# Long scans over a feature-major tile, their multipliers in PSUM, and the layer 1 sum on TensorE

## The chip, the cores and the metric

The kernel runs on one core of one Trainium2 chip. The metric is the device time of one execution in microseconds (us), from the first to the last instruction; lower is better. All data are float32 unless said otherwise. The engines are called as in the profile: PE (TensorE), PEld (its weight loads), DVE (VectorE), ACT (ScalarE), POOL (GpSimd, which here issues the indirect DMAs) and SP (which issues the plain ones).

## The reference

A graph network of two layers over 12500 nodes and 200000 edges sorted by receiver `dst`. Each layer's result is added to its input and normalised.

```
# layer 0: attention over incoming edges, 4 heads of 16 features
h = (x @ W_node).reshape(n, H, HD)
attn = a_src[src] + a_dst[dst] + edge_attr_16 @ W_edge       # a_src = h . attn_src, a_dst = h . attn_dst
attn = where(attn >= 0, attn, 0.2 * attn)
attn_max = zeros(n, H).at[dst].max(attn)
attn = exp(attn - attn_max[dst])
attn_sum = zeros(n, H).at[dst].add(attn)
out = zeros(n, H, HD).at[dst].add(h[src] * (attn / (attn_sum[dst] + 1e-8)))
x = layernorm(x + layernorm(out + h) * gamma + beta)
# layer 1: a message per edge, its mean per receiver
hid = relu(concat(x[src], x[dst], edge_attr_32) @ W1 + b1)   # 160 -> 128
agg = segment_sum(hid @ W2 + b2, dst) / max(degree, 1)
x = layernorm(x + agg + (x @ Wn + bn))
```

## The kernel before

**Lanes.** The edges are padded to 128 lanes of 1568 columns (`LANE`): partition p holds edges 1568 p to 1568 p + 1567, sorted by receiver. A sum or maximum per receiver is a running one along the lane: `same` (128 x 1568) is 1 where an edge has the receiver of the one before it and 0 where a new receiver starts. The running rows are stored to DRAM (`rows0`, `rows1`), and the last row of each node is later fetched from there. What a receiver has in the lanes before is carried over by small matmuls.

**Stages, in order of time.** (1) The node table `table0` (h, source terms) is made, and the edges of each node are counted. (2) Layer 0 over the edges: `K0` = 49 chunks of `C0` = 32 columns. (3) Layer 0 over the nodes, 10 steps: combine, normalise, project to `table1s` (source part of W1) and `table1d` (receiver part), and scatter the latter to the first edge of each receiver in `recv_term`, which is zero elsewhere. (4) Layer 1 over the edges: `K1` = 196 chunks of `C1` = 8 columns. (5) Layer 1 over the nodes.

**Gathers.** A column of 128 source rows is fetched by one indirect DMA of POOL: L433 and L450 for layer 0 (`gather0`, `gather_columns`, 1440 + 128 of them), L525 for layer 1 (`gather1`, 1568). Each layer has a ring of four slots (`G0`, `G1`), and POOL fills a slot again when its last user has raised a semaphore: `rows0_ready` (the last scan of a chunk) in layer 0, `relu_done` in layer 1. L484 fetches last rows of nodes (`gather_last`), L489 scatters receiver terms.

**A chunk of layer 0** (`turn0` of DVE, L1025 to L1060). DVE adds three terms to a score (L1035, L1038), takes the leaky relu (L1040), scans the maximum per head (L1044, four scans of 32), forms the arguments of two exponentials (L1047 to L1049), which ACT computes in one pass (L748). DVE multiplies the second by `same` (L1051), the gathered features by the first (L1053, 128 x 2048, in place), and runs 64 + 4 scans of 32 columns (L1057, L1059), each `row = decay * row_before + term`, into `R0[par]`; SP stores that (1152 KB). PE multiplies the edge attributes (4 small matmuls); SP also writes 2 MB of zeros to `recv_term` a chunk.

**A chunk of layer 1** (`turn1` of DVE, L1178 to L1215). SP loads the receiver terms into one of four `X1` buffers. DVE runs two recurrences over the eight columns, one instruction of 128 x 128 for a column each, the two interleaved: the receiver rows (L1191, `X[u] = same[u] * X[u-1] + X[u]`), and the sums of the chunk before (L1197, the same form on `H1`). Then it adds the receiver rows to the gathered rows (L1209, 128 x 1024) and the PE result, which is in PSUM (L1214, two of 128 x 512); ACT takes relu into `H1` (L832), SP stores `H1` (512 KB). PE multiplies the edge attributes with a block-diagonal W1 (two matmuls of 128x512 f32, L565, a helper's line).

**What sets the order** is written by hand: each engine has its own loop, with semaphores between them, and SP's loop per chunk (`chunk0`, `chunk1`) loads and stores in a fixed order, so a load stands behind the store before it.

## Time and profile before

| | |
|---|---|
| runs | 4751.53, 4755.95, 4757.55 us; median 4755.95 |
| profiled execution, span | 4755.7 us |
| busy: POOL, DVE, PE, PEld, ACT | 3565.7, 2619.7, 1308.6, 660.9, 493.5 us |
| layer 0 gathers of the loop | 358.5 to 2257.6 us |
| layer 1 gathers | 2589.9 to 4585.5 us |
| mean granted TensorE clock | 0.554 |

Times in the trace count from the first instruction. A row of a group gives the line, engine, operation, output <- inputs, shapes, count, busy time, the mean of one instruction in ns, and behind the last bar the idle time of the engine just before these instructions, with what ended it ("issue": nothing that the profile shows). A timeline row gives start, duration, line and, in brackets, the idle time before. A fp32 matmul appears as two MATMUL instructions.

### The profile page before, as it was taken

Reading aid. Unit: us, or ns where it says so; the run is one execution under the profiler, and the core shown is the slowest. Engines: PE = TensorE matmul, PEld = TensorE weight load, DVE = VectorE, ACT = ScalarE, POOL = GpSimd, SP = SyncE. Lnnn points to the kernel's source line nnn. Section 1 sums busy time; section 2 is a strip of 40 time slices with the busy share of each in tenths; the row PEclk is TensorE's granted clock in tenths of the full one; section 3 lists DMA queues with packets and bytes.
Section 4 is the critical chain, followed back from the end, with each engine's and each line's share of the span. In section 5 each row is a group of like instructions: output and inputs, shape, how many; then the busy total and the mean of one; then the engine's idle time right before and its main releaser. Section 6 shows DMA issues by size and latency. Waiting matters only on the chain. (4 is left out here: it accounts for less than half of the span.)

```text
span 4755.7 us, 33914 instructions
## 1 busy us (share of the span) xinstructions
PE 1308.6 (28%) x3363; PEld 660.9 (14%) x3363; DVE 2619.7 (55%) x8568; ACT 493.5 (10%) x1011; POOL 3565.7 (75%) x3558
## 2 busy tenths in 40 slices
PE   7600000000000000000575333333333333333336
PEld 4300000000000000000453111111111111111126
DVE  6545443344433444433774666666666666666645
ACT  4500000000000000000232111111111111111101
POOL 5777777777777777777676777777777777777766
PEclk9855555555555555555555655655665556556655
DMA  3034333333333333333232555555555555555532
GB/s 124 10 112 160 100 105 118 118 117 112 93 118 118 118 118 99 106 118 113 85 121 94 169 171 167 165 170 170 162 170 171 161 170 171 166 166 171 170 104 63
DMA packets 240932, 622.28 MB, mean 131 GB/s; under 512 B 74956, under 2 KB 102543, under 8 KB 221521
## 3 DMA queue, kind: packets, MB, share of 16 engines
q1 hardware_dynamic: 127568, 443.81, 28.2%
q0 software_dynamic: 113280, 177.74, 14.7%
q14 instruction: 78, 0.63, 0.0%
q8 instruction: 6, 0.10, 0.0%
HBM read 328.11 MB, written 293.29 MB: 131 GB/s over the span
## 5 line engine op out<-in xcount | busy, mean ns | idle before, releaser
L525 POOL DMA_INDIRECT edge_arena<-table1s,ix x1568 | 1518.0, 968 | 477.9 <-issue 435.2
L433 POOL DMA_INDIRECT edge_arena<-table,ix x1440 | 1460.5, 1014 | 438.9 <-issue 438.9
L565 PE MATMUL ps<-w1e_bd,edge_terms 128*128 128x512 f32 x784 | 725.1, 1080 | 1264.4 <-DMA edge_terms<-e32g_d 1264.4
L1191 DVE SCALAR_TENSOR_TENSOR edge_arena<-edge_arena,same 128x128 f32<-128x128 f32 x1568 | 542.0, 346 | 263.6 <-issue 189.1
L565 PE MATMUL ps<-we_bd,edge_terms 128*128 128x32 f32 x392 | 93.6, 403 | 1864.1 <-DVE score L1038 1803.8
L1035 DVE TENSOR_TENSOR score<-edge_arena,node_wide 128x128 f32<-128x128 f32 x49 | 14.2, 291 | 1066.0 <-DMA edge_arena<-table,ix 1065.6
L1057 DVE TENSOR_TENSOR_SCAN edge_arena<-wq,edge_arena 128x32 f32<-128x32 f32 x3136 | 586.8, 268 | 1.8
L1197 DVE SCALAR_TENSOR_TENSOR edge_arena<-edge_arena,same 128x128 f32<-128x128 f32 x1568 | 539.7, 344 | 1.5 <-ACT edge_arena L832 1.2
L565 PEld LDWEIGHTS ps<-w1e_bd,edge_terms 128*128 128x128 f32 x784 | 229.0, 322 | 1759.2 <-issue 1759.2
L1209 DVE TENSOR_TENSOR edge_arena<-edge_arena 128x1024 f32<-128x1024 f32 x196 | 240.9, 1229 | 404.5 <-DMA edge_arena<-table1s,ix 404.5
L832 ACT ACTIVATE edge_arena<-edge_arena 128x1024 f32<-128x1024 f32 x196 | 207.0, 1056 | 1800.9 <-DVE edge_arena L1214 1800.9
L565 PEld LDWEIGHTS ps<-we_bd,edge_terms 128*128 128x128 f32 x392 | 87.2, 328 | 1870.5 <-DVE score L1038 1769.3
L484 POOL DMA_INDIRECT node_arena<-rows,end_ix x200 | 210.5, 1053 | 96.5 <-issue 59.4
L1214 DVE TENSOR_TENSOR edge_arena<-edge_arena,ps 128x512 f32<-128x512 f32 x392 | 251.8, 683 | 6.7
L748 ACT ACTIVATE wq<-expo 128x256 f32<-128x256 f32 x49 | 20.4, 416 | 2028.3 <-DVE expo L1049 2028.3
L450 POOL DMA_INDIRECT edge_arena<-table,ix x128 | 143.3, 1120 | 39.0 <-issue 39.0
L489 POOL DMA_INDIRECT recv_term<-node_arena,start_ix x100 | 120.6, 1206 | 48.4 <-issue 32.7
L565 PE MATMUL ps<-node_arena 128*128 128x512 bf16 (+1 forms) x800 | 146.3, 332 | 28.5 <-DVE row_base L953 16.4
L565 PE MATMUL ps<-w1n,node_arena 128*128 128x128 f32 (+1 forms) x400 | 133.9, 488 | 24.1 <-ACT node_arena L777 24.1
L455 POOL DMA_INDIRECT dst_term<-a_dst,start_idx x100 | 104.9, 1049 | 30.5 <-issue 30.5
L742 ACT ACTIVATE node_arena<-ps,node_half 128x1057 bf16<-128x1057 f32 x100 | 114.3, 1143 | 63.4 <-PE ps L565 58.9
L1053 DVE TENSOR_TENSOR edge_arena<-edge_arena,wq 128x2048 f32<-128x2048 f32 x49 | 111.9, 2284 | 0.0
(177 smaller groups left out, 1462.5 us busy)
## 6 DMA issues: line engine op xcount, KB each, us to landing
recv_term<-zeros SPq DMA_DIRECT2D x98, 1024.0 KB, 9.1
edge_arena<-recv_term SPq DMA_DIRECT2D x196, 512.0 KB, 4.1
rows<-edge_arena SPq DMA_DIRECT2D x196, 512.0 KB, 5.1
rows<-edge_arena SPq DMA_DIRECT2D x49, 1152.0 KB, 4.4
edge_arena<-table,ix POOLq DMA_INDIRECT x1568
edge_terms<-e32g_d SPq DMA_DIRECT2D x196, 128.0 KB, 4.8
edge_arena<-table1s,ix POOLq DMA_INDIRECT x1568
edge_terms<-e16g_d SPq DMA_DIRECT2D x49, 256.0 KB, 9.2
```

The source lines that it names most:

```text
L433: pool.indirect_dma_start(G0[slot][:, u, :], None, table0, bass.IndirectOffsetOnAxis(ap=ix[slot][:, u:u + 1], axis=0)).then_inc(gathered0[ ...
L450: pool.indirect_dma_start(G0[slot][:, u, :], None, table0, bass.IndirectOffsetOnAxis(ap=ix[slot][:, u:u + 1], axis=0)).then_inc(gathered0[ ...
L484: pool.indirect_dma_start(RG[r][:, b, :], None, rows, bass.IndirectOffsetOnAxis(ap=end_ix[r][:, b:b + 1], axis=0)).then_inc(done[r], 16)
L489: pool.indirect_dma_start(recv_term, bass.IndirectOffsetOnAxis(ap=start_ix[r][:, b:b + 1], axis=0), PDs[r][:, b, :], None, bounds_check=NE ...
L525: pool.indirect_dma_start(G1[slot][:, u, :], None, table1s, bass.IndirectOffsetOnAxis(ap=ix[slot][:, u:u + 1], axis=0)).then_inc(gathered1 ...
L565: return pe.matmul(out_, lhsT, rhs, start=start, stop=stop)
L832: act.activation(H1[s], G1[s], ACT.Relu).then_inc(relu_done, 1)
L1057: scan(R[:, :, f], wq[:, :, H + f // HD], G[:, :, f], before[:, f:f + 1], ALU.mult, ALU.add)
L1191: stt(X[:, u, :], X[:, u - 1, :] if u else Xb[:, C1 - 1, :], same[:, bass.ds(c * C1 + u, 1)], X[:, u, :], ALU.mult, ALU.add).then_inc(dv1, 1)
L1197: a = stt(Hc[:, u, :], Hc[:, u - 1, :] if u else Hb[:, C1 - 1, :], same[:, bass.ds(c * C1 - C1 + u, 1)], Hc[:, u, :], ALU.mult, ALU.add)
L1209: tt(G1[s], G1[s], X, ALU.add).then_inc(recv_used, 1)
L1214: last = tt(part_g, part_g, ps[:, 2 * s + g, :], ALU.add)
```

## The change

In both layers the many short instructions of a recurrence become scans over a long free axis. A tile is laid out feature-major, with one more column in front of each feature's columns: the seed, which is the last column of the chunk before. A scan `state = mult * state + data` runs over all features in one instruction; the multiplier at a seed column is 0, which starts the next feature.

**Layer 0.** `F0[par]` (4 heads x 17 x 33, 17 being 16 features and the sum of weights) lies in the node arena, in two copies. The maximum is one scan of 132 elements with multipliers `hold0` in SBUF (a copy of `same` by ACT). ACT writes the weights (exp of 128 elements) to PSUM, again into `F0`'s 17th row, and the decays, spread over 17 rows (2176 elements), to PSUM (`decay`, from bank 2 on); the product with `same` is gone, the argument being lowered by up to 1000 instead (`cut`, ALU.min). DVE multiplies features by weights (2048 elements, now SBUF times PSUM, into `F0`), and runs one scan of 2244 elements, multipliers in PSUM. ACT copies `F0` and the maxima into `R0` for the store. POOL's slot is free after the multiply (`g0_free`) rather than after the scans.

**Layer 1.** A chunk is 16 columns (`C1`), so there are 98. There is one `X1` buffer (1 MB a load) in the node arena; ACT copies it feature-major into `F1[0]` or `F1[1]`, DVE scans it in five pieces (4 of 510 elements, 1 of 136), with multipliers in PSUM (`hold1`, written by ACT). PE adds the three terms in PSUM banks 2 to 5: four edge matmuls, four of the identity with the gathered rows, four of the identity with the scanned receiver rows (read with a stride). ACT's relu reads PSUM and writes `F1[2]` or `F1[3]`; DVE scans that too, and ACT copies it into `H1`, which is stored (1 MB). Both adds of DVE (L1209, L1214) are gone. SP and POOL wait for DVE to leave the node arena (`arena_free`).

The diff, cut to its core, in the order globals and tiles, SP, PE, ACT (layer 0, then 1), DVE (layer 0, then 1):

```diff
-C1 = 8
+C1 = 16
+CUT = 1000.0
...
+        decay = ps_flat[:, 2 * BANK:2 * BANK + H * HF * T0]
+        weight = ps[:, 7, 0:H * C0].rearrange("p (h t) -> p h t", t=C0)
...
+        T1 = C1 + 1
+        F1 = [part(node_arena, i * HID * T1, HID * T1) for i in range(4)]
+        XF1, HF1 = (0, 1), (2, 3)
+        X1 = part(node_arena, 4 * HID * T1, C1, HID)
+        FEATS = BANK // T1
+        hold1 = [ps[:, r, 0:FEATS * T1] for r in range(2)]
+        PIECES1 = [(f * T1, min(HID, f + FEATS) * T1) for f in range(0, HID, FEATS)]
...
+            def chunk1(c, s, loads=True, follows=True, stores=True):
+                if follows:
+                    sp.wait_ge(xf_ready, c + 1)
+                    sp.dma_start(X1, recv_p[:, bass.ds(c * C1 + C1, C1), :]).then_inc(recv_in, 16)
                 if loads:
+                    sp.wait_ge(edge1_mm, c * 2 + 4)
+                    sp.dma_start(edge_terms[s][:, :, :], e32g[:, bass.ds(c * 4 + 4 * RING1, 4), :]).then_inc(e32_in[s], 16)
+                if stores:
+                    store1(c - 1, 1 - s % 2)
...
             def edge1(c, s, it):
+                r = s % 2
                 pe.wait_ge(e32_in[s], it * 16 + 16)
-                pe.wait_ge(pre_ready, c + 1)
-                for g in range(2):
-                    last = mm(ps[:, 2 * s + g, :], edge_terms[s][:, g, :], w1e_bd[:, :])
-                last.then_inc(edge1_mm, 1)
+                pe.wait_ge(half_used[0], c + 1)
+                for g in range(4):
+                    mm(ps[:, 2 + g, :], edge_terms[s][:, g, :], w1e_bd[:, :], True, False)
+                pe.wait_ge(gathered1[s], it * (16 * C1) + 16 * C1)
+                for g in range(4):
+                    mm(ps[:, 2 + g, :], ident[:, :], G1[s][:, 4 * g:4 * g + 4, :].rearrange("p t f -> p (t f)"), False, False)
+                pe.wait_ge(scanned_x, c + 1)
+                for g in range(4):
+                    recv = F1_f[XF1[r]][:, :, 1 + 4 * g:5 + 4 * g].rearrange("p f t -> p t f")
+                    last = mm(ps[:, 2 + g, :].rearrange("p (t f) -> p t f", f=HID), ident[:, :], recv, False, True)
+                    if g % 2:
+                        last.then_inc(edge1_mm, 1)
...
+            def turn0(c, slot, copies, holds):
+                act.wait_ge(weight_arg, c + 1)
+                act.activation(weight, expo[:, 0, :, :], ACT.Exp).then_inc(weights_ready, 1)
+                act.wait_ge(rows0_ready, c + 1)
+                act.activation(F0_h[par][:, :, HD, 1:T0], expo[:, 0, :, :], ACT.Exp)
+                act.wait_ge(decay_arg, c + 1)
+                act.wait_ge(scanned0, c + 1)
+                act.activation(decay_h[:, :, :, 1:T0], expo[:, 1, :, :].unsqueeze(2).to_broadcast([P, H, HF, C0]),
+                               ACT.Exp).then_inc(decay_ready, 1)
...
+                act.wait_ge(scanned0, c + 2)
+                act.wait_ge(rows0_stored[par], (c - par) * 8 + 16)
+                act.activation(heads(R0[par][:, :, 0:D]), F0_h[par][:, :, 0:HD, 1:T0], ACT.Copy)
...
+            def turn1(c, s, copies=True, follows=True, c_later=True):
+                if follows:
+                    act.wait_ge(led_x, c + 1)
+                    act.wait_ge(edge1_mm, c * 2 + 2)
+                    recv_1(c + 1, 1 - r)
+                if c_later:
+                    rows_1(c - 1, 1 - r)
+                    if follows:
+                        hold_1(c + 1, 1 - r)
+                act.wait_ge(edge1_mm, c * 2 + 4)
...
+                act.activation(F1_f[HF1[r]][:, :, 1:T1].rearrange("p f t -> p t f"),
+                               ps[:, 2:6, :].rearrange("p a (t f) -> p (a t) f", f=HID), ACT.Relu).then_inc(half_used[0], 1)
...
-                tt(wq[:, :, H:2 * H], wq[:, :, H:2 * H], wide(same_c.unsqueeze(2), [P, C0, H]), ALU.mult)
-                tt(feats, feats, wide(wq[:, :, 0:H].unsqueeze(3), [P, C0, H, HD]), ALU.mult).then_inc(dv0, 1)
-                for f in range(D):
-                    scan(R[:, :, f], wq[:, :, H + f // HD], G[:, :, f], before[:, f:f + 1], ALU.mult, ALU.add)
+                scan(flat(M), flat(hold0[par]), flat(score), 0.0, ALU.mult, ALU.max).then_inc(dv0, 1)
...
+                tt(F[:, :, 0:HD, 1:T0], G[:, :, 0:D].rearrange("p t (h d) -> p h d t", d=HD),
+                   wide(weight.unsqueeze(2), [P, H, HD, C0]), ALU.mult).then_inc(g0_free, 1)
...
+                scan(F0[par], decay, F0[par], 0.0, ALU.mult, ALU.add).then_inc(scanned0, 1)
...
+            def scan1(F, hold, done):
+                for lo, hi in PIECES1:
+                    last = scan(F[:, lo:hi], hold[:, 0:hi - lo], F[:, lo:hi], 0.0, ALU.mult, ALU.add)
+                last.then_inc(done, 1)
...
+            def turn1(c, s, it, first=False):
+                    dve.tensor_copy(F1_f[XF1[r]][:, :, 0:1], F1_f[XF1[1 - r]][:, :, C1:T1]).then_inc(led_x, 1)
+                    lead1(c - 1, 1 - r)
...
+                scan1(F1[XF1[r]], hold1[r], scanned_x)
+                if not first:
+                    sums1(c - 1, 1 - r)
```

## Rows read from the trace of the kernel before

**Rows 1.** The page, part 1: busy us (share of the span) x instructions.

```profile
PE 1308.6 (28%) x3363; PEld 660.9 (14%) x3363; DVE 2619.7 (55%) x8568; ACT 493.5 (10%) x1011; POOL 3565.7 (75%) x3558
```

**Rows 2.** Groups of the whole span, POOL's three largest kinds of gather.

```profile
L525 POOL DMA_INDIRECT edge_arena<-table1s,ix x1568 | 1518.0, 968 | 477.9 <-issue 435.2 <-ACT edge_arena L832 42.1 <-ACT ix L726 0.6
L433 POOL DMA_INDIRECT edge_arena<-table,ix x1440 | 1460.5, 1014 | 438.9 <-issue 438.9
...
L450 POOL DMA_INDIRECT edge_arena<-table,ix x128 | 143.3, 1120 | 39.0 <-issue 39.0
```

**Rows 3.** Groups of POOL in a stretch of layer 0 with DVE idle.

```profile
L433 POOL DMA_INDIRECT edge_arena<-table,ix x17 | 16.0, 943 | 5.2 <-issue 5.2
```

**Rows 4.** Timeline of layer 0: a gather beside the multiply of L1053.

```profile
489.97 2.28 DVE L1053 TENSOR_TENSOR edge_arena<-edge_arena,wq 128x2048 f32<-128x2048 f32 x1
490.33 2.74 POOL L433 DMA_INDIRECT edge_arena<-table,ix  x1 [0.30 <-issue]
```

**Rows 5.** Timeline before layer 0's chunks: a gather beside L1021's scans.

```profile
299.83 13.61 DVE L1021 TENSOR_TENSOR_SCAN node_wide<-same,lane_rows,node_wide 128x1568 f32<-128x1568 f32 x4 [76.48 <-DMA node_wide<-dst_term]
300.22 3.85 POOL L450 DMA_INDIRECT edge_arena<-table,ix  x1 [0.30 <-issue]
```

**Rows 6.** Timeline of stages 4 and 5: gathers beside DVE instructions that read PSUM.

```profile
2907.25 1.28 DVE L1214 TENSOR_TENSOR edge_arena<-edge_arena,ps 128x512 f32<-128x512 f32 x2
...
2908.33 0.95 POOL L525 DMA_INDIRECT edge_arena<-table1s,ix  x1 [0.31 <-issue]
...
4650.02 0.82 DVE L1244 TENSOR_TENSOR node_arena<-ps,inv_deg 128x640 f32<-128x640 f32 x1
4650.53 0.94 POOL L484 DMA_INDIRECT node_arena<-rows,end_ix  x1 [0.30 <-issue]
```

**Rows 7.** Groups of the whole span: the short scans of layer 0.

```profile
L1057 DVE TENSOR_TENSOR_SCAN edge_arena<-wq,edge_arena 128x32 f32<-128x32 f32 x3136 | 586.8, 268 | 1.8
```

**Rows 8.** Timeline of the end of layer 0's edge stage.

```profile
2256.61 0.94 POOL L433 DMA_INDIRECT edge_arena<-table,ix  x1 [0.30 <-issue]
2259.08 0.29 DVE L1035 TENSOR_TENSOR score<-edge_arena,node_wide 128x128 f32<-128x128 f32 x1 [23.76 <-DMA edge_arena<-table,ix]
...
2264.51 11.97 DVE L1057 TENSOR_TENSOR_SCAN edge_arena<-wq,edge_arena 128x32 f32<-128x32 f32 x64
2276.40 0.82 DVE L1059 TENSOR_TENSOR_SCAN edge_arena<-wq,edge_arena 128x32 f32<-128x32 f32 x4
...
2281.74 0.94 POOL L484 DMA_INDIRECT node_arena<-rows,end_ix  x1 [24.18 <-DMA rows<-edge_arena]
```

**Rows 9.** Groups of ACT, whole span: relu and the exponentials.

```profile
L832 ACT ACTIVATE edge_arena<-edge_arena 128x1024 f32<-128x1024 f32 x196 | 207.0, 1056 | 1800.9 <-DVE edge_arena L1214 1800.9
...
L748 ACT ACTIVATE wq<-expo 128x256 f32<-128x256 f32 x49 | 20.4, 416 | 2028.3 <-DVE expo L1049 2028.3
```

**Rows 10.** Timeline before layer 1: eight edge matmuls in a row.

```profile
2567.72 8.82 PE L565 MATMUL ps<-w1e_bd,edge_terms 128*128 128x512 f32 x16 [4.31 <-DMA edge_terms<-e32g_d]
```

**Rows 11.** Windows: stretch, engines' busy us (x), PEclk, DMA share, GB/s.

```profile
2567.70:2571.10 3.40, 3.38 (x4) 1.51 (x5) 3.40 (x1) 0.00 (x0) 3.40 (x1) 0.50 0.30 90
2571.10:2576.50 5.40, 5.40 (x13) 2.09 (x11) 5.37 (x2) 0.00 (x0) 5.09 (x2) 0.99 0.04 12
```

**Rows 12.** The page, part 6: a DMA of 1 MB, issue to landing.

```profile
recv_term<-zeros SPq DMA_DIRECT2D x98, 1024.0 KB, 9.1
```

**Rows 13.** Timeline where layer 1's edge stage begins.

```profile
2571.68 6.82 DVE L1169 TENSOR_TENSOR node_wide<-node_wide,node_arena 128x6400 f32<-128x6400 f32 x1
...
2588.59 0.98 POOL L531 DMA_INDIRECT edge_arena<-table1d,ends_i  x1 [0.31 <-issue]
```

**Rows 14.** Timeline of the end of layer 1's edge stage.

```profile
4584.57 0.94 POOL L525 DMA_INDIRECT edge_arena<-table1s,ix  x1 [0.30 <-issue]
4587.18 1.23 DVE L1209 TENSOR_TENSOR edge_arena<-edge_arena 128x1024 f32<-128x1024 f32 x1 [3.73 <-DMA edge_arena<-table1s,ix]
...
4597.49 0.94 POOL L484 DMA_INDIRECT node_arena<-rows,end_ix  x1 [11.97 <-DMA rows<-edge_arena]
```

More of the change, by code:

```diff
@@ L205, in build @@
         rstd = part(node_arena, 11716, NC)
+        HF = HD + 1
+        F0 = [part(node_arena, r * H * HF * T0, H * HF * T0) for r in range(2)]
+        F0_h = [f.rearrange("p (h d t) -> p h d t", d=HF, t=T0) for f in F0]
+        ps_flat = ps[:, :, :].rearrange("p a b -> p (a b)")
+        decay = ps_flat[:, 2 * BANK:2 * BANK + H * HF * T0]
+        decay_h = decay.rearrange("p (h d t) -> p h d t", d=HF, t=T0)
+        weight = ps[:, 7, 0:H * C0].rearrange("p (h t) -> p h t", t=C0)
+        cut = part(node_arena, 9296, LANE)
         big_a = part(node_arena, 4160, H, P)
@@ L407, in _ @@
             pool.memset(zeros[:, :], 0.0)
+            for r in range(2):
+                pool.memset(hold0[r][:, :, :], 0.0)
             pool.memset(upto[:, 0:1], 0.0)
@@ L743, in _, with hold @@
                                    scale=-1.0, accum_out=sign_sum[:, bass.ds(j * 2 + i, 1)]).then_inc(row_free[i], 1)
[L746 to L748 removed]
+            def hold(c, par):
+                act.activation(hold0[par][:, :, 1:T0], same[:, bass.ds(c * C0, C0)].unsqueeze(1).to_broadcast([P, H, C0]),
+                               ACT.Copy).then_inc(hold0_ready, 1)
@@ L752, in _ @@
+                act.activation(R0[par][:, :, MCOL:ROW].rearrange("p t h -> p h t"), peak[par][:, :, 1:T0],
+                               ACT.Copy).then_inc(rows0_ready, 1)
+            act.wait_ge(seeds_zero, 1)
+            for par in range(2):
+                hold(par, par)
             with act.Fori(0, (K0 - 5) // RING0) as it:
                 for slot in range(RING0):
-                    turn0(it * RING0 + slot, slot, True)
+                    turn0(it * RING0 + slot, slot, True, True)
@@ L876, in _ @@
             dve.sem_inc(cc_free, 1)
-            dve.sem_inc(pre_ready, RING1)
+            for h in range(2):
+                dve.sem_inc(half_used[h], 1)
             dve.sem_inc(agg_used, 2)
@@ L1053, in turn0 @@
-                tt(feats, feats, wide(wq[:, :, 0:H].unsqueeze(3), [P, C0, H, HD]), ALU.mult).then_inc(dv0, 1)
-                dve.wait_ge(dv0, c * 4 + 4)
-                dve.wait_ge(rows0_ready, c + 1)
-                for f in range(D):
-                    scan(R[:, :, f], wq[:, :, H + f // HD], G[:, :, f], before[:, f:f + 1], ALU.mult, ALU.add)
-                for h in range(H):
-                    last = scan(R[:, :, ZCOL + h], wq[:, :, H + h], wq[:, :, h], before[:, ZCOL + h:ZCOL + h + 1], ALU.mult, ALU.add)
@@ L1231, in _ @@
             dve.wait_ge(carry1_mm, 1)
+            for r in range(2):
+                dve.wait_ge(rows1_stored[r], 16 * (K1 // 2 + 1))
             dve.tensor_copy(rgT[0][:, 0:P], ps[:, 0, 0:P]).then_inc(carry1_cp, 1)
```

247 lines of the change are left out of this document (135 added, 112 removed).

## The prediction

> **What bounds the kernel now.** I read the page's first part and its groups first. POOL is busy 75% of the span [rows 1], but that counts only the 0.94 to 1.01 us that each indirect DMA takes to generate; behind each of them stand about 0.305 us of issue in which POOL does nothing else. With both, the layer 1 gathers take 1518.0 + 477.9 = 1995.9 us, the layer 0 gathers of the loop 1460.5 + 438.9 = 1899.4 us and the first 128 gathers 143.3 + 39.0 = 182.3 us [rows 2]: 4077.6 of 4755.7 us. The reader is to see that the idle time in these rows is all "issue" (the 42.1 us put down to ACT in layer 1 are the same 0.3 us gaps, since 477.9 / 1568 = 0.305): POOL never waits for DVE, ACT, PE or a landing. So DVE's 2619.7 us, which the change cuts most, are worth nothing as such. What is worth something is what DVE does to the gathers.
>
> For that I take a gather alone. In a stretch of layer 0 in which DVE is idle, 17 gathers have a mean of 943 ns [rows 3]; over all of the layer the mean is 1014 ns, in layer 1 it is 968 ns [rows 2]. The timeline shows where the rest comes from: the gather of 490.33 starts while the feature multiply of L1053 runs (489.97 to 492.25), and takes 2.74 us; it ends at 493.07, 0.82 us after the multiply has ended [rows 4]. The same with a scan: the first L1021 scan (1568 elements) starts at 299.83, and the gather that starts 0.39 us later takes 3.85 us [rows 5]. So a gather that begins during a DVE instruction with both inputs in SBUF stops 0.12 us into its work until DVE is done, and then needs its other 0.82 us. A gather that began just before such an instruction isn't held. Where one of the inputs is in PSUM it is different: the gather of 4650.53 begins inside L1244 (PSUM times SBUF, 4650.02 to 4650.84) and takes 0.94 us where the rule above would give 1.13; the one of 2908.33 begins 0.2 us before the L1214 pair (SBUF plus PSUM) is done and takes 0.95 us [rows 6].
>
> The Trainium skill (SBUF — State Buffer, section "Who interferes with whom") says that a DVE instruction with two SBUF inputs contends with a GpSimd instruction that reads SBUF, and that one with at most one SBUF input outside the 2-port modes doesn't; our rows agree. In the same list it reports a probe in which tensor_tensor did not stall descriptor generation. That sentence speaks against any gain here: without the stalls there would be nothing to win, and the time would be the one that I give below for "nothing to win". The 2.74 us row decides against it.
>
> **The change, part by part.** The span is 4755.7 us, the median of the runs 4755.95: what I take off the one I take off the other.
>
> Layer 0, gathers. Excess over the free gather: 1460.5 − 1440 × 0.943 = 102.6 us, and 143.3 − 128 × 0.943 = 22.6 us for the first 128, of which most belongs to L1021 and the counting stage and stays. The multiply of L1053 runs 49 times, 46 of them beside the gathers of the loop and three beside the first 128. It can cost 0 (no gather begins in it) to some 2.2 us, and cost 1.8 at 490.33; taking 2.28 less half of the 1.25 us between gathers, 1.65, it carries 46 × 1.65 = 76 us of the 102.6, and the rest is small delays by the L1057 scans; of the first 128 it carries 3 × 1.65 = 5 us. In the new kernel the multiply reads its weights from PSUM, and the 68 short scans become one of 4 × 17 × 33 = 2244 elements with its multipliers in PSUM. By rows 6 neither holds a gather. Left are two-SBUF instructions of 128 elements as before, which did next to nothing, and one scan of 132 elements; I leave 4 us for them (between 0, and 0.5 us a chunk = 24 us). Gain: 102.6 + 5 − 4 = 103.6 us.
>
> Does the new work fit behind a chunk of gathers, 32 × (0.943 + 0.305) = 39.9 us? Scan: L1057 takes 268 ns for 32 elements [rows 7] and the four L1021 scans 13.61 us, 3.40 us each for 1568 [rows 5], so (3.40 − 0.19) / 1536 = 2.09 ns an element (0.19 us being the start-to-start time of the short ones, 11.97 / 64 [rows 8]), and 2244 elements take 4.9 us. With the multiply (2.3) and eight small instructions DVE has about 10 us a chunk. ACT: L832 takes 1056 ns for 1024 elements and L748 416 ns for 256 [rows 9]: 0.83 ns an element and 0.2 us. Two exponentials of 128, the decay of 2176, the copies of 2048 and 2 × 128, the hold and the indices come to 0.3 + 0.3 + 2.0 + 1.9 + 0.6 + 0.5 = 5.6 us. Both hidden; if that cover were gone, each us of either would cost 49 us.
>
> Layer 1, gathers. Excess: 1518.0 − 1568 × 0.943 = 39.4 us, from the 32 short instructions a chunk with a pointer scalar and two SBUF inputs. The new scans read their holds from PSUM, the two adds of DVE are gone. I leave 1 us (0 to 10): gain 38.4 us.
>
> Layer 1, does it fit behind 16 gathers, 16 × 1.248 = 20.0 us? DVE: 2 × 2176 elements in 10 scans, 2 × (4.55 + 5 × 0.12) = 10.3 us, and two seeds. ACT: three passes of 2048 (1.9 us each), a hold of 480 (0.6) and the indices (0.2): 6.5 us. PE: four edge matmuls, four for the gathered rows, four for the receiver rows, all 128x512 f32. The trace has eight such matmuls back to back (16 instructions, 8.82 us) [rows 10]: the first 3.4 us at a granted clock of 0.50 (1.2 GHz), in which four instructions are done, then 0.99 (2.4 GHz) with the other twelve in 5.4 us [rows 11]. A matmul is two instructions: 1.7 us at the lower level and 0.87 at the higher. Twelve cost 20.4 us or 10.4 us. PSUM has one buffer for them, so relu (1.9 us) and the hand-overs (0.3) come on top: 12.6 us at the higher clock. After the gathers of a chunk have landed PE does eight matmuls without a pause, longer than the 3.4 us after which the clock rose; I take two at the lower level and six at the higher, 8.6 us, then relu, then four edge matmuls: 14 us of 20. Matmuls that read the receiver rows with a stride of 17 elements stand in no row; at twice the time they add 3.5 us and stay hidden. The receiver rows now have one buffer, and SP loads chunk c+1 only behind ACT's copy of chunk c and behind the store of chunk c−2, which waits for ACT again. 1 MB takes 9.1 us to land at the worst [rows 12]; with recv copy, rows copy, hold and relu (6.3 us) this loop takes some 16 us, under 20. POOL's slots: four of 16 columns, freed by relu; it is three chunks (60 us) ahead.
>
> Where layer 1 begins, SP and POOL now wait for DVE to leave the node arena. DVE's last pass there ends at 2578.50 and POOL comes to the first gather of layer 1's stage at 2588.59 [rows 13], so I cost it at nothing (0 to 2 us); without these 10 us it would cost what DVE is late.
>
> The end of layer 0. Before: the last gather begins at 2256.61, DVE starts at 2259.08 and its last scan ends at 2277.22, and POOL goes on at 2281.74, 4.5 us later with the store between [rows 8]. New, from 2259.08: three small (1.0), the scan of 132 (0.5), the subtraction (0.3), ACT's exponential (0.4), multiply (2.3), scan (4.9), ACT's copies (2.4), store (4.5): 16.3 us in place of 22.7, gain 6.4 us.
>
> The end of layer 1. Before: the last gather begins at 4584.57, DVE starts at 4587.18, POOL goes on at 4597.49: 10.3 us [rows 14]. New: eight matmuls from the lower clock (8.6), relu (2.1), five scans (5.2), ACT's copy into the rows (2.0), a store of 1 MB (4.4, like the 1.15 MB of layer 0): 22.3 us with 0.2 for hand-overs. Loss 12.2 us (10 at the higher clock throughout, 17 at the lower).
>
> Sum: 4755.7 − 103.6 − 38.4 − 6.4 + 12.2 = **4619.5 us**, by 2.9% less. The node stages are left alone: nothing in their code changes.
>
> **The rivals.**
> 1. A scan with its multipliers in PSUM still holds gathers. Rows 6 show tensor_tensor alone, and not a scan; what speaks for it is only that the rows are short instructions of another kind. Price: as L1053 cost 1.6 us with 2.28, a scan of 4.9 us costs about 4.3, × 49 = 209 us; in layer 1 ten scans a chunk, each holding the gather that begins in it by half of 1.06 us, some 6 gathers a chunk: 2.8 × 98 = 275 us. 4619.5 + 209 + 275 = 5104 us, slower than before. It decides as soon as half of the scans hold a gather (142 us gained against 484). Chance 0.07.
> 2. PE stays at its lower clock and becomes the bound of layer 1: 20.4 + 1.9 + 0.3 = 22.6 us a chunk against 20.0, 98 × 2.6 = 255 us, 4619.5 + 255 + 5 = 4880 us, slower. It decides from 20 us a chunk for twelve matmuls and a relu. Against it stands the 0.99 of [rows 11] after 3.4 us of the same matmuls. The Trainium skill (TensorE: Matmul & The Clock Gate, Part 1) says that half rate is the default and activity releases it, which would end this case by itself: a PE that is the bound is busy all the time. Chance 0.03.
> 3. The loop through the one receiver buffer and the hand-overs of ACT, DVE and SP is longer than 20 us: at 22 us a chunk 98 × 2 = 196 us, 4815 us, slower; at 20.5 us 4670 us. It needs landings of over 13 us for 1 MB, which no row shows. Chance 0.06, half of it slower than before.
> 4. Nothing to win: the stalls come back at other places, or don't hang on DVE's inputs at all. Then the ends alone count: 4755.7 − 6.4 + 12.2 = 4761.5, within 0.2%. Chance 0.03.
>
> **How the numbers follow.** The forecast has 0.81. Its own bounds: 24 us more for the small layer 0 instructions, 9 for layer 1, 5 for the end at the lower clock, some us of what I couldn't see; below, 4 + 1 for what I left and 2 for the end. That is 4610 to 4655. The range goes to 4675 to take in the mild half of case 3 and hand-overs that I mis-sized, and down to 4600. Faster by over 0.2% (about what a measurement of this kernel can tell from no change): 0.81 + 0.03 (the mild half of case 3) = 0.84; slower: 0.07 + 0.03 + 0.03 = 0.13; between: case 4, 0.03.
>
> **What would show it.** Right: the mean of the gathers at 943 to 950 ns in both layers, all idle time before them still "issue" at 0.305 us; a gather that begins during a long scan takes 0.94 us. DVE's busy time falls by over a third with no effect of its own. Between the last gather of layer 1 and the first of the last stage about 25 us in place of 12.9. Wrong: gathers of 3 to 5 us beside the 2244-element scan (case 1); idle time of POOL released by ACT's relu, with PE at 0.50 (case 2) or with PE waiting for the scan of the receiver rows (case 3).

## The result, and the profile after

The changed kernel takes 4681.82 us (median; 4679.21 to 4683.91) against 4754.67 us for the kernel before in the same measurement: a ratio of 0.9849, with a 95% interval of 0.9835 to 0.9863. It is faster by 1.5%, where 2.9% were forecast, and 6.8 us above the upper end of the range. The profiled execution has a span of 4680.6 us, 75.1 less than before. The medians here and below leave out one execution, of the kernel of experiment 5, which took 9870.74 us where its other three took 4625 to 4635.

The page's first part and POOL's largest groups (columns as in [rows 1] and [rows 2]):

```profile
PE 2215.4 (47%) x4911; PEld 966.5 (21%) x4931; DVE 1959.1 (42%) x2644; ACT 1758.3 (38%) x1403; POOL 3425.6 (73%) x3560
...
L557 POOL DMA_INDIRECT edge_arena<-table1s,ix x1568 | 1480.9, 944 | 486.3 <-issue 478.2
L465 POOL DMA_INDIRECT edge_arena<-table,ix x1440 | 1361.3, 945 | 438.8 <-issue 438.8
```

POOL's waits in the whole span (us in total, times, longest):

```profile
POOL edge_arena L557 <- issue: 478.2, 1546, 1.5
POOL edge_arena L465 <- issue: 438.8, 1440, 0.3
POOL node_arena L516 <- DMA rows<-edge_arena: 95.4, 2, 73.8
```

The gathers did what was forecast: their means are 944 and 945 ns in place of 968 and 1014 [rows 2]. The time went into the last line: before the last stage POOL stands for 73.8 us, where it stood for 11.97 [rows 14]. The account of the span, before to after:

| Term | forecast | measured | from |
|---|---|---|---|
| Gathers of layer 0, with the first 128 | −103.6 | −104.9 | 1460.5 to 1361.3, and 143.3 to 137.6 (137.6 is the group of L482) |
| Gathers of layer 1, busy | −38.4 | −37.1 | 1518.0 to 1480.9 |
| Waits within layer 1's gathers | 0 | +8.4 | 477.9 to 486.3 |
| Wait at the end of layer 0 | −6.4 | −2.6 | 24.2 to 21.6 (95.4 − 73.8) |
| Wait at the end of layer 1 | +12.2 | +61.8 | 11.97 to 73.8 |
| Sum | −136.2 | −74.4 | span: −75.1 |

Two gathers beside the new work of DVE in layer 0 (timeline: start, us, engine, line):

```profile
996.03 3.83 DVE L1170 TENSOR_TENSOR node_arena<-edge_arena,ps 128x2048 f32<-128x2048 f32 x1
997.10 0.95 POOL L465 DMA_INDIRECT edge_arena<-table,ix  x1 [0.30 <-issue]
...
999.95 4.83 DVE L1175 TENSOR_TENSOR_SCAN node_arena<-ps,node_arena 128x2244 f32<-128x2244 f32 x1
1000.85 0.94 POOL L465 DMA_INDIRECT edge_arena<-table,ix  x1 [0.30 <-issue]
```

Both begin inside an instruction with its multipliers in PSUM, and neither is held, against 2.74 us in [rows 4].

Where the 73.8 us come from is seen in layer 1's loop (timeline; POOL and the weight loads left out):

```profile
3501.64 3.80 ACT L928 ACTIVATE node_arena<-ps 128x2048 f32<-128x2048 f32 x1 [3.15 <-PE ps L602]
...
3503.34 0.33 SPq L401 DMA_DIRECT2D node_arena<-recv_term  x1
3505.49 5.91 PE L602 MATMUL ps<-w1e_bd,edge_terms 128*128 128x512 f32 x8 [3.89 <-ACT node_arena L928]
...
3511.24 3.60 PE L602 MATMUL ps<-edge_arena,ident 128*128 128x512 f32 x8
3513.61 3.83 ACT L908 ACTIVATE node_arena<-node_arena 128x2048 f32<-128x2048 f32 x1 [7.76 <-DMA node_arena<-recv_term]
3514.67 7.41 PE L602 MATMUL ps<-node_arena,ident 128*128 128x512 f32 x8
...
3522.12 3.80 ACT L928 ACTIVATE node_arena<-ps 128x2048 f32<-128x2048 f32 x1 [0.64 <-PE ps L602]
```

Read the starts. From relu to relu it is 20.48 us: relu 3.80, edges 5.75, gathered rows 3.43, receiver rows 7.41, and 0.09 between them. Each waits for the one before it, as they share one set of PSUM banks. POOL needs 19.98 us for 16 gathers. PE and ACT thus fall 0.5 us behind in each of 98 chunks. For most of the layer nobody waits for that: POOL is ahead by the slots of the ring. The lag comes due at the end of the layer, when everything still in the ring has to pass through the loop, and from about the 80th chunk on POOL itself waits a little (the 8.4 us). Over the whole layer, from the first relu at 2515.7 to the last at 4505.2, the loop has a mean of 20.51 us.

Groups of the new passes (whole span; busy, mean ns); L809 and the scan L1175 came out as forecast, the others did not:

```profile
L602 PE MATMUL ps<-w1e_bd,edge_terms 128*128 128x512 f32 x784 | 580.0, 909 | 382.3 <-ACT node_arena L928 377.4 <-DMA edge_terms<-e32g_d 4.9
...
L908 ACT ACTIVATE node_arena<-node_arena 128x2048 f32<-128x2048 f32 x98 | 375.3, 3830 | 524.7 <-DMA node_arena<-recv_term 485.9 <-DVE node_arena L1314 38.4 <-ACT node_arena L928 0.4
L928 ACT ACTIVATE node_arena<-ps 128x2048 f32<-128x2048 f32 x98 | 372.3, 3799 | 324.5 <-PE ps L602 324.5
...
L817 ACT ACTIVATE edge_arena<-node_arena 128x2048 f32<-128x2048 f32 x49 | 189.8, 3874 | 319.7 <-DVE node_arena L1175 319.7
...
L809 ACT ACTIVATE ps<-expo 128x2176 f32<-128x2176 f32 x49 | 97.4, 1988 | 6.9 <-DVE expo L1165 1.8
...
L1175 DVE TENSOR_TENSOR_SCAN node_arena<-ps,node_arena 128x2244 f32<-128x2244 f32 x49 | 236.7, 4831 | 4.4
L1170 DVE TENSOR_TENSOR node_arena<-edge_arena,ps 128x2048 f32<-128x2048 f32 x49 | 187.8, 3833 | 0.0
```

L908 and L928 write a tile in SBUF with 17 elements from one to the next, L817 writes one with 72 (a row of `R0`), and they take 1.85 to 1.89 ns an element; L809, which writes neighbours, takes 0.91 and is at the forecast. The same on DVE: L1170, which reads the gathered rows 72 elements apart, takes 3.83 us where L1053 took 2.28 [rows 4].

TensorE's clock in the stretches of that loop (us, busy us of PE, PEld, DVE, ACT, POOL, PEclk, DMA share, GB/s):

```profile
3505.50:3509.00 3.50, 3.50 (x4) 1.50 (x5) 3.42 (x4) 0.22 (x1) 2.59 (x4) 0.50 0.94 318
3509.00:3511.20 2.20, 2.20 (x5) 0.94 (x4) 1.91 (x5) 0.00 (x0) 1.59 (x3) 0.78 0.78 294
3511.20:3514.60 3.40, 3.40 (x9) 1.52 (x8) 0.00 (x0) 0.99 (x1) 2.64 (x3) 1.00 0.30 89
```

After the 3.89 us in which PE stands for relu it starts again at 0.50 (1.2 GHz), so the edge matmuls, not the gathered ones, pay for the clock. It is so in every chunk: the edge matmuls are busy 580.0 us in 98 chunks, 5.92 us each, and 5.91 in the one above.

### The profile page after: what moved, and what is told of

Same layout as the page of the kernel before. It is cut to its first block, busy times and chain, and to the rows that moved or that the text cites. A ratio compares the mean times of both kernels' runs of the same rounds, so it can differ in the third digit from the quotient of the medians.

```text
span 4680.6 us, 24041 instructions
## 1 busy us (share of the span) xinstructions
PE 2215.4 (47%) x4911; PEld 966.5 (21%) x4931; DVE 1959.1 (42%) x2644; ACT 1758.3 (38%) x1403; POOL 3425.6 (73%) x3560
## 4 chain that ended last, share of the span: by engine, by line
POOL 39%; PE 37%; issue 13%; ACT 8%; DVE 1%; DMA 1%; SPq 0%; POOLq 0%; DVEq 0%; ACTq 0%
PE ps L602 37%; POOL edge_arena L465 29%; ACT node_arena L928 8%; POOL edge_arena L482 3%; POOL node_arena L516 2%; POOL dst_term L487 2%; POOL edge_arena L557 1%; POOL recv_term L521 1%; DMA node_arena<-rows,end_ix 0%; PE ps L756 0%; DMA table<-node_arena 0%; DMA edge_arena<-table1s,ix 0%; SPq L313 0%; PE ps L682 0%; DVE node_arena L1175 0%
## 5 line engine op out<-in xcount | busy, mean ns | idle before, releaser
L557 POOL DMA_INDIRECT edge_arena<-table1s,ix x1568 | 1480.9, 944 | 486.3 <-issue 478.2
L465 POOL DMA_INDIRECT edge_arena<-table,ix x1440 | 1361.3, 945 | 438.8 <-issue 438.8
L1296 DVE TENSOR_TENSOR_SCAN node_arena<-ps,node_arena 128x510 f32<-128x510 f32 (+1 forms) x980 | 956.2, 1043 | 1027.1 <-ACT ps L903 792.7
L602 PE MATMUL ps<-node_arena,ident 128*128 128x512 f32 x784 | 726.4, 1083 | 0.0
L908 ACT ACTIVATE node_arena<-node_arena 128x2048 f32<-128x2048 f32 x98 | 375.3, 3830 | 524.7 <-DMA node_arena<-recv_term 485.9
L928 ACT ACTIVATE node_arena<-ps 128x2048 f32<-128x2048 f32 x98 | 372.3, 3799 | 324.5 <-PE ps L602 324.5
L913 ACT ACTIVATE edge_arena<-node_arena 128x2048 f32<-128x2048 f32 x98 | 370.6, 3782 | 12.2 <-DVE node_arena L1296 12.2
L602 PE MATMUL ps<-edge_arena,ident 128*128 128x512 f32 x784 | 354.4, 595 | 38.2 <-DMA edge_arena<-table1s,ix 38.2
L516 POOL DMA_INDIRECT node_arena<-rows,end_ix x200 | 212.7, 1064 | 155.7 <-DMA rows<-edge_arena 95.4
L817 ACT ACTIVATE edge_arena<-node_arena 128x2048 f32<-128x2048 f32 x49 | 189.8, 3874 | 319.7 <-DVE node_arena L1175 319.7
L602 PEld LDWEIGHTS ps<-node_arena,ident 128*128 128x128 f32 x784 | 159.5, 203 | 457.5 <-issue 457.5
L1175 DVE TENSOR_TENSOR_SCAN node_arena<-ps,node_arena 128x2244 f32<-128x2244 f32 x49 | 236.7, 4831 | 4.4
L602 PEld LDWEIGHTS ps<-edge_arena,ident 128*128 128x128 f32 x784 | 149.4, 191 | 228.0 <-issue 186.6
L1170 DVE TENSOR_TENSOR node_arena<-edge_arena,ps 128x2048 f32<-128x2048 f32 x49 | 187.8, 3833 | 0.0
L482 POOL DMA_INDIRECT edge_arena<-table,ix x128 | 137.6, 1075 | 39.0 <-issue 39.0
```

Source lines behind the costliest of these rows:

```text
L465: pool.indirect_dma_start(G0[slot][:, u, :], None, table0, bass.IndirectOffsetOnAxis(ap=ix[slot][:, u:u + 1], axis=0)).then_inc(gathered0[ ...
L482: pool.indirect_dma_start(G0[slot][:, u, :], None, table0, bass.IndirectOffsetOnAxis(ap=ix[slot][:, u:u + 1], axis=0)).then_inc(gathered0[ ...
L516: pool.indirect_dma_start(RG[r][:, b, :], None, rows, bass.IndirectOffsetOnAxis(ap=end_ix[r][:, b:b + 1], axis=0)).then_inc(done[r], 16)
L557: pool.indirect_dma_start(G1[slot][:, u, :], None, table1s, bass.IndirectOffsetOnAxis(ap=ix[slot][:, u:u + 1], axis=0)).then_inc(gathered1 ...
L602: return pe.matmul(out_, lhsT, rhs, start=start, stop=stop)
L817: act.activation(heads(R0[par][:, :, 0:D]), F0_h[par][:, :, 0:HD, 1:T0], ACT.Copy)
```

## The experiments

The theory after the result: layer 1's loop through the PSUM banks is 20.5 us and hence the bound; what made it so is the strided access to SBUF, in relu and in PE's receiver matmuls. The rivals: the loop through the receiver buffer (SP's load, ACT's copy, the scan), and the granted clock alone. Besides, the gain of layer 0 is to be tied to its cause.

**1. Relu in two halves**, each with its semaphore, so that the next edge matmuls start behind the first.

```diff
-                pe.wait_ge(half_used[0], c + 1)
                 for g in range(4):
+                    if g % 2 == 0:
+                        pe.wait_ge(half_used[g // 2], c + 1)
...
+                for h in range(2):
+                    act.wait_ge(edge1_mm, c * 2 + 3 + h)
+                    act.activation(F1_f[HF1[r]][:, :, 1 + 8 * h:9 + 8 * h].rearrange("p f t -> p t f"),
+                                   ps[:, 2 + 2 * h:4 + 2 * h, :].rearrange("p a (t f) -> p (a t) f", f=HID),
+                                   ACT.Relu).then_inc(half_used[h], 1)
```

> One edit to the changed kernel, with the same result: relu of layer 1 in two passes of 1024 (PSUM banks 2-3, then 4-5), each raising its own semaphore, and PE's edge matmuls of the next chunk wait for the half that they write. Theory A (the bound of layer 1 is the loop PE 16.58 us, relu 3.80, hand-over 0.1 through the one PSUM buffer, 20.48 us a chunk against POOL's 19.98): the loop falls to PE's own time, about 15 to 16.5 us, the consumers no longer fall behind, and the wait of POOL before the last stage falls from 73.8 to about 30 us: 4680 - 44 - 8 = 4628 us. Rival B (the loop through the one receiver buffer, SP's order and ACT's two copies is the bound): the halves take only 1.9 us from every second chunk; at most 20 us, 4660 or more. Rival C (only the lower clock of PE holds it): PE no longer pauses for relu and so keeps 2.4 GHz; the edge matmuls would fall from 5.75 to 3.4 us, which alone gives 18.1 us and the same total as A, but with relu still in the loop.

Measured: 4632.86 us for 4628 expected, ratio 0.9741 (0.9725 to 0.9757). POOL's waits:

```profile
POOL edge_arena L557 <- issue: 477.8, 1568, 0.3
...
POOL node_arena L516 <- DMA rows<-edge_arena: 51.3, 2, 29.8
```

All 1568 idle times in layer 1 are issue again, and the last wait falls from 73.8 to 29.8 us. Not all of these 44.0 us are the lag: behind the last matmul only the second half of relu is left on the path,

```profile
4459.55 1.98 ACT L930 ACTIVATE node_arena<-ps 128x1024 f32<-128x1024 f32 x1 [1.59 <-PE ps L602]
```

in place of 3.80 us, which is worth 1.8. The lag is the other 42.2 and the 8.5 within the gathers, 50.7 us, where a loop of 20.51 us against 19.98 makes 52 in 98 chunks. The edit gives back 49 of the 62 us that were missing, and nothing about POOL or the gathers was touched. Rival B, which had at least 4660 us, is false. On C, the clock, this run says nothing, as both theories gave the same total.

**2. Layer 0 alone**: the changed layer 0 with the layer 1 of before.

> Layer 0 as changed, layer 1 as before (chunks of 8, DVE's recurrences, adds on DVE). By the traces the layer 0 part gains 99.3 us in the loop's gathers, 5.7 in the first 128 and 2.6 at the end of the stage: 4755.7 - 107.6 = 4648 us, faster than the whole change (4681.8). If instead the layer 1 part also gained over before, this one would come out above 4681.8 us.

Measured: 4644.08 us, 4 us under the expectation, ratio 0.9765 (0.9748 to 0.9781). Two groups of POOL:

```profile
L541 POOL DMA_INDIRECT edge_arena<-table1s,ix x1568 | 1514.4, 966 | 477.8 <-issue 436.3 <-ACT edge_arena L871 39.9 <-ACT ix L742 1.5
L449 POOL DMA_INDIRECT edge_arena<-table,ix x1440 | 1362.9, 946 | 438.7 <-issue 438.7
```

So the layer 1 part, as built, loses 4681.8 − 4644.1 = 37.7 us, although its gathers are faster; with relu in halves it wins 11.2.

**3. Two receiver buffers**, everything else as in the changed kernel.

```diff
-        X1 = part(node_arena, 4 * HID * T1, C1, HID)
+        X1 = [part(node_arena, 4 * HID * T1 + i * (W1R + HID), C1, HID) for i in range(2)]
...
-                    sp.dma_start(X1, recv_p[:, bass.ds(c * C1 + C1, C1), :]).then_inc(recv_in, 16)
+                    sp.dma_start(X1[s % 2], recv_p[:, bass.ds(c * C1 + 2 * C1, C1), :]).then_inc(recv_in[s % 2], 16)
```

> One edit to the changed kernel, with the same result: two receiver buffers in place of one, so that a load is issued a whole chunk earlier. Theory A: the loop through PSUM and relu stays 20.48 us a chunk, and the time stays at 4680 us within 5 us. Rival B (the receiver loop is the bound): the wait for the landing (485.9 us in ACT, 88 times) goes, the chunk falls under 20 us, and the time to about 4630 us.

Measured: 4687.1 us, ratio 0.9849 (0.9833 to 0.9866), the same ratio as the changed kernel's; the time is 7 us above the 4680 expected, 2 more than the 5 allowed, in another measurement. Waits of ACT (L929 is relu) and of POOL:

```profile
ACT node_arena L929 <- PE ps L603: 736.4, 98, 22.9
...
POOL node_arena L517 <- DMA rows<-edge_arena: 95.4, 2, 73.8
```

ACT's wait for the receiver rows to land was 485.9 us and is 14.6 now; its wait for PE rose from 324.5 to 736.4 instead, and the end stayed at 73.8. The 485.9 us was the largest wait of ACT in the loop, and was worth nothing. The receiver loop, which the forecast had as its rival, was not the bound.

**4. Relu writes neighbouring elements.** Same amount of work and the same waits; the order of the features is left out, so the sums are of the wrong values.

```diff
-                act.activation(F1_f[HF1[r]][:, :, 1:T1].rearrange("p f t -> p t f"),
-                               ps[:, 2:6, :].rearrange("p a (t f) -> p (a t) f", f=HID), ACT.Relu).then_inc(half_used[0], 1)
+                act.activation(F1_f[HF1[r]][:, :, 1:T1],
+                               ps[:, 2:6, :].rearrange("p a b -> p (a b)").rearrange("p (f t) -> p f t", t=C1),
+                               ACT.Relu).then_inc(half_used[0], 1)
```

> One edit to the changed kernel: relu of layer 1 writes its 2048 results in runs of 16 neighbours (it leaves out the transposition to feature-major order, so the sums are of the wrong values). Theory A with a stride as the cause of ACT's 1.85 ns an element: relu takes 1.9 us in place of 3.80, the loop 18.6 us, under POOL's 20.0, and the time falls to about 4630 us. If the source in PSUM, not the stride of the write, costs the time: relu stays 3.8 us and the time 4680 us.

Measured: 4630.97 us, ratio 0.9736 (0.9717 to 0.9756). The group of relu:

```profile
L928 ACT ACTIVATE node_arena<-ps 128x2048 f32<-128x2048 f32 x98 | 183.9, 1876 | 276.4 <-PE ps L602 276.3
```

1876 ns is the 1.9 us that the forecast had put in, and with it the layer runs at POOL's pace: all 1568 idle times of POOL are issue, and the last wait is 28.6 us. The price of the strided write is shown. The run also decides on the clock alone. The edge matmuls are still slow,

```profile
L602 PE MATMUL ps<-w1e_bd,edge_terms 128*128 128x512 f32 x784 | 552.5, 871 | 197.7 <-ACT node_arena L928 192.8 <-DMA edge_terms<-e32g_d 4.9
```

871 ns an instruction against 909, and POOL doesn't wait: the setback of the clock by itself doesn't make the loop too long.

**5. PE reads the receiver rows as neighbours.**

```diff
-                    recv = F1_f[XF1[r]][:, :, 1 + 4 * g:5 + 4 * g].rearrange("p f t -> p t f")
-                    last = mm(ps[:, 2 + g, :].rearrange("p (t f) -> p t f", f=HID), ident[:, :], recv, False, True)
+                    recv = F1[XF1[r]][:, g * BANK:g * BANK + BANK]
+                    last = mm(ps[:, 2 + g, :], ident[:, :], recv, False, True)
```

> The same kernel as e4_receiver_unit_stride once more (the first time the kernel before itself took 5641 us on that chip in place of 4755, with waits that belong to no instruction, so that the few per cent in question drowned). PE reads the receiver rows as neighbouring elements; this leaves out their right order. Theory A (the loop through the one set of PSUM banks is the bound of layer 1): 4628 to 4633 us, no wait of POOL in the loop. Rival (the receiver loop of 20.15 us is right behind it): 4648 us or above.

Measured: 4633.21 us (4625.26 to 4635.43), ratio 0.9730 (0.9712 to 0.9748). This is just above the 4628 to 4633 of the theory, in a measurement in which the kernel before took 4763.5 us, 9 more than in 1. The group of the receiver matmuls, and POOL's waits:

```profile
L602 PE MATMUL ps<-node_arena,ident 128*128 128x512 f32 x784 | 352.4, 592 | 0.0
```

```profile
POOL edge_arena L557 <- issue: 477.8, 1568, 0.3
...
POOL node_arena L516 <- DMA rows<-edge_arena: 49.5, 2, 27.8
```

The mean of one instruction falls from 1083 to 592 ns, and again POOL doesn't wait. Either of the two strides, taken away alone, frees the loop: it was over by 0.5 us only, and they are worth 1.9 and 3.9 us of it. The edge matmuls, at 878 ns, still pay for the clock. Edges at the upper level (3.43 us for 5.75) would by the same sum leave a loop of 18.2 us; that is an estimate, no run has it. The rival, a receiver loop close behind (20.15 us), is refuted here and in 1: once PE and ACT have slack, it doesn't hold POOL.

The kernels of 5, 6 and 7 also ran on another chip, on which the kernel before took 5641 us (5600 to 5678), and there alone 8 ran. In each of these kernels ACT's relu waited 496 to 785 us in all on that chip for a release that the trace can't place, and POOL behind it 47 to 65 times for up to 18 us. Their ratios were 0.9713 for 5, 0.9853 for 6 and 0.9667 for 7, with intervals of 0.004 to 0.005 to either side. Waits of that size hide what is looked for; why that chip was slower stays open. The times given for 5, 6 and 7 are from a chip on which the kernel before took 4763.5 us.

**6. The multipliers of layer 0 back in SBUF**, with the long scan and the multiply as they are.

```diff
-        decay = ps_flat[:, 2 * BANK:2 * BANK + H * HF * T0]
+        decay = part(node_arena, 5760, H * HF * T0)
-        weight = ps[:, 7, 0:H * C0].rearrange("p (h t) -> p h t", t=C0)
+        weight = part(node_arena, 8064, H, C0)
...
+            for r in range(TABS):
+                dve.wait_ge(tab_st[r], 16 * len(range(r, len(TABG), TABS)))
```

The added wait stands once, ahead of layer 0, where the table's stores leave that part of the arena.

> The same kernel as e5_multipliers_in_sbuf once more, for the same reason: layer 0 with its long scan and multiply, weights and decays in SBUF. On the first chip the gathers of the loop rose only from a mean of 1.037 to 1.147 us, 158 us in all. Theory (every gather that begins in an instruction of D us with two SBUF inputs is held and costs D - 0.75 us, in scan and multiply): 4980 to 5050 us. Rival with half of it (only one of the two, or only the gathers that begin early in it, are held): 4682 + 150 to 160 = 4830 to 4845 us. Rival that the place of the multipliers is nothing: 4682 us.

Measured: 4992.07 us, ratio 1.0482 (1.0466 to 1.0498), within the theory's numbers. The timeline of a chunk:

```profile
1027.78 3.85 DVE L1172 TENSOR_TENSOR node_arena<-edge_arena,node_arena 128x2048 f32<-128x2048 f32 x1
1028.66 3.74 POOL L465 DMA_INDIRECT edge_arena<-table,ix  x1 [0.30 <-issue]
...
1031.73 4.83 DVE L1177 TENSOR_TENSOR_SCAN node_arena<-node_arena 128x2244 f32<-128x2244 f32 x1
1032.71 4.60 POOL L465 DMA_INDIRECT edge_arena<-table,ix  x1 [0.30 <-issue]
```

The gather of 1028.66 ends at 1032.40, 0.77 us after the multiply; the next at 1037.31, 0.75 after the scan. Together they cost 2.80 + 3.66 = 6.5 us a chunk; over the loop the gathers take 286 us more, and the first 128 of them 21 more (158.3 for 137.6), which with the rest of 3 us makes up the 310 us between this kernel and the changed one. On the slower chip the ratio of 0.9853 was far from what the theory gives, but the same gathers were held there (3.76 us beside the multiply, 4.59 beside the scan), and those of the loop came to 1652.0 us, here to 1647.4. The instructions last as long as in the changed kernel (3.85 and 4.83): DVE is neither faster nor slower for it, only POOL is. Long instructions without the PSUM operand would have made the kernel slower by 5%, so with the long instructions the gain of layer 0 hangs on the place of the multipliers; short scans with their multipliers in PSUM no run has. The Trainium skill (SBUF — State Buffer, section "Who interferes with whom") has both sides as rules: a DVE instruction with two inputs in SBUF contends with a GpSimd instruction that reads SBUF, and one with at most one, outside the 2-port modes, doesn't. The trace agrees for the multiply and for the scan: 3.74 and 4.60 us here, 0.95 and 0.94 in the changed kernel.

**7. Halves, and the receiver rows before the gathered rows.** Kernel 1, with the two groups of matmuls in PE's program exchanged (`scanned_x` is waited for first, `gathered1` second).

> The same kernel as e8_halves_receiver_first once more, for the same reason: relu in two halves, and PE adds the receiver rows before the gathered rows. Theory: only the end of layer 1 changes, by the 7.4 us of the receiver matmuls: 4625.5 us (4623 to 4628). Rival (PE waits for the scanned receiver rows in every chunk, the ring fills, POOL waits for relu): 4633 us or more.

Measured: 4631.2 us, ratio 0.9723 (0.9710 to 0.9737). POOL's waits:

```profile
POOL edge_arena L557 <- issue: 478.2, 1568, 0.3
...
POOL node_arena L516 <- DMA rows<-edge_arena: 44.4, 2, 22.7
```

The last wait is 22.7 us, 7.1 less than in 1, as expected of matmuls of 7.4 us. The time itself missed the 4623 to 4628 us expected. The times, 4631.2 here and 4632.9 in 1, are from two measurements, with the kernel before at 4763.5 and 4754.9, and in the profiled executions the last gather of layer 1 ends 4.6 us later here than in 1, before the place where the two differ (4449.90 against 4445.27). Their ratios overlap, so the 7 us stand in the wait and are not settled in the whole. The rival is false: PE waits 28.9 us in all for the scanned rows, and POOL not at all. Of the versions with the right result this one has the lowest ratio, 2.8% under the kernel before.

**8. The stride by itself.** Behind the last stage ACT, DVE and PE each work on 256 elements that lie 1, 2, 4, 5, 8 and 17 apart in SBUF, each stride at least twice. One execution, of 5469.79 us, on the slower chip; only single instructions are read from it.

> The changed kernel with a measurement behind its last stage, which adds its own time (some 40 to 60 us) at the end: ACT, DVE and PE each work on 256 f32 elements a partition in SBUF whose neighbours lie 1, 2, 4, 5, 8 and 17 elements apart: ACT writes, then reads them, DVE writes them in a copy, then reads them as one input of a multiply, PE reads them as the moving operand of a matmul with 128x128. Theory of a step: the full rate up to a certain stride, then about the double and no more with a longer stride; by the rows of the changed kernel (1.85 against 0.83 to 0.9 ns an element on ACT) 256 elements at stride 17 take ACT 0.2 to 0.3 us more than at stride 1, and stride 5 or 8 the same as 17. The Trainium skill (SBUF - State Buffer, the note on cachelines) puts the step between 4 and 5 f32 elements, and names no price. Theory of distance: the time grows steadily with the stride, at 4 and 8 already by a quarter and a half of what it is at 17. For PE the step would be 1.08 us against 0.6 us for two instructions' half of 512 elements, so some 0.25 us more on 256.

The timeline, ACT's writes at strides 1, 2, 4 and 17, and DVE's multiply with one input at strides 2, 4 and 17 (one of two or three each):

```profile
5450.55 0.42 ACT L1011 ACTIVATE edge_arena<-probe_in 128x256 f32<-128x256 f32 x1
5451.00 0.43 ACT L1013 ACTIVATE edge_arena<-probe_in 128x256 f32<-128x256 f32 x1
5451.94 0.66 ACT L1017 ACTIVATE edge_arena<-probe_in 128x256 f32<-128x256 f32 x1
5456.83 0.65 ACT L1031 ACTIVATE edge_arena<-probe_in 128x256 f32<-128x256 f32 x1
```

```profile
5457.53 0.43 DVE L1493 TENSOR_TENSOR probe_out<-edge_arena,probe_in 128x256 f32<-128x256 f32 x1
5457.99 0.62 DVE L1495 TENSOR_TENSOR probe_out<-edge_arena,probe_in 128x256 f32<-128x256 f32 x1
5462.54 0.61 DVE L1509 TENSOR_TENSOR probe_out<-edge_arena,probe_in 128x256 f32<-128x256 f32 x1
```

It is a step: stride 2 costs next to nothing, 4 already the whole price (0.24 us for 256 elements on ACT, 0.19 on DVE), and 5, 8 and 17 cost no more. ACT's reads take 0.42, 0.44, then 0.65 to 0.68 us. DVE's copies, which write with the stride, take 0.29, 0.29 to 0.30, then 0.39 to 0.41: the same step, but at only 0.11 us half the price of the multiply's. The expectation had 4 still on the cheap side. The Trainium skill (SBUF — State Buffer, the note on cachelines) explains the step by lines of 16 bytes, in each of which at least two accesses are wanted, and says in the same note that a stride of 4 f32 is free. The first fits (stride 2 has two elements to a line), the second doesn't: at 4, 0.66 us.

For PE the starts of the weight loads, one pair a matmul of 256 columns, at strides 1, 2 and 17 (two each):

```profile
5445.37 0.30 PEld L609 LDWEIGHTS ps<-edge_arena,ident 128*128 128x128 f32 x2 [1.39 <-DVEq L1448]
5446.13 0.30 PEld L609 LDWEIGHTS ps<-edge_arena,ident 128*128 128x128 f32 x2 [0.46 <-PE ps L609]
...
5449.20 0.50 PEld L609 LDWEIGHTS ps<-edge_arena,ident 128*128 128x128 f32 x2 [0.78 <-PE ps L609]
5450.48 0.50 PEld L609 LDWEIGHTS ps<-edge_arena,ident 128*128 128x128 f32 x2 [0.78 <-PE ps L609]
...
5464.94 0.50 PEld L609 LDWEIGHTS ps<-edge_arena,ident 128*128 128x128 f32 x2 [0.81 <-PE ps L609]
5466.25 0.50 PEld L609 LDWEIGHTS ps<-edge_arena,ident 128*128 128x128 f32 x2 [0.81 <-PE ps L609]
```

The first pair, stride 1, is 0.76 us apart at a granted clock of 1.00. By stride 2 the clock was at 0.50; there stride 2 takes 1.28 us and strides 4 and 17 take 1.31; stride 1 was not measured at that level. So this probe missed the expected 0.25 us: at 1.2 GHz the step from stride 2 to 4 costs PE almost nothing. What it costs at 2.4 GHz is in the loop above, 7.41 us for eight instructions of 512 columns, or 1.81 ns a column, in place of 3.43 to 3.6. That is the same 1.8 to 1.9 ns an element as on ACT and in DVE's multiply.

## Why the prediction was wrong, point by point

- **POOL is the bound, and only what DVE does to its gathers counts.** Right: DVE's busy time fell by 661 us, and the gathers fell by 142.0 us for a forecast of 142.0. Each layer was off by 1.3 us, one way and the other; that the sum came out to the tenth is luck. Experiment 6 ties the gain of layer 0 to the PSUM operand.
- **"A scan with its multipliers in PSUM still holds gathers"** (rival 1) is false: 0.94 us inside the 4.83 us scan. **"PE stays at its lower clock"** (rival 2) is false as it was put, the clock is 1.00 for over half of the loop; but it does fall back in every chunk. **"Nothing to win"** (rival 4) is false.
- **"Three passes of 2048 (1.9 us each)".** This is the first of the two terms that failed in the sum of the layer 1 loop; the other is the clock of the edge matmuls, below. The price came from L832 and L748 [rows 9], which read and write neighbours; the new passes turn the tile and take 3.8 us (experiment 4: 1.88 without the turn). The forecast had noticed the stride for PE ("at twice the time they add 3.5 us and stay hidden", measured +3.9) and not for ACT, where relu is in the same loop. The same miss on DVE's multiply (2.3 forecast, 3.83) and on ACT's copy at the end of layer 0 (1.9, 3.87) is 3.5 us, which turns the gain of 6.4 there into 2.9; 2.6 were measured.
- **"14 us of 20".** With the 3.5 us for the strided matmuls it should have read 17.5 of 20. Measured 20.5: relu +1.9; edges 5.75 in place of 3.5, since relu's pause sets the clock back and not the wait for the gathers; gathered and receiver rows 10.8 in place of 12.1 (for the same reason); hand-overs 0.1. A sum that leaves 2.5 us of slack in 20 was carried on as one that leaves 6. Relu's 1.9 us alone would have left the loop at 19.4 us, under POOL's 19.98; only together with the 2.25 us of the edges is it over. What is shown is that the loop is over by 0.5 us and that taking relu's 1.9 or the matmuls' 3.9 out of it frees POOL (experiments 4 and 5); the share of the clock rests on the sum.
- **Rival 3** ("the loop through the one receiver buffer and the hand-overs ... at 20.5 us 4670 us") has the right size and the wrong place. Its 20.5 us did occur, through the PSUM banks; the second buffer of experiment 3 changed nothing. Its price of 49 us a half microsecond is about what was lost (42.2 + 8.4). Its condition, "it needs landings of over 13 us", kept its chance at 0.06: it priced one way of reaching 20 us and left out longer passes. The signs of being wrong were put in the wrong place as well: they name idle time of POOL released by relu, and what came was one long wait released by the store of the rows, behind the loop.
- **The end of layer 1**, forecast at 22.3 us (its terms make 22.5, and the loss of 12.2 goes by that) and a wait of 24. With the lag away (experiment 1) the wait is 29.8: relu's second half 2.0 in place of 2.1, but receiver rows 7.4 and the copy 3.8, 7.4 − 3.5 and 3.8 − 2.0, together 5.7 us more than was counted. The changed kernel, with its relu in one piece, has another 1.8 there, 31.6 us.
- **Range.** All of the miss is in the layer 1 loop and the two ends: 42.2 + 8.4 for the lag, 7.4 for the end of layer 1 without it (a loss of 19.6 for 12.2), 3.8 for the end of layer 0, 61.8 us of 61.8 (−136.2 to −74.4).

## What to carry to other kernels

Price every pass from a row with the same access pattern, not only of the same size: a transposing copy or relu on ACT, a multiply on DVE and a moving operand of PE at the upper clock cost 1.81 to 1.89 ns an element a partition here, at strides of 17 and 72 f32; the probe puts the step on ACT and DVE at a stride of four or less, and above two. Where several engines pass one buffer in a ring, write the loop out as a sum and hold it against the bound's pace: half a microsecond over in 98 rounds cost 51 us, most of it at the end where no wait in the loop points at it. The largest wait of an engine in such a loop (486 us here) says nothing until the loop that it belongs to is the longest.
